# Convolution taps loaded by tap rows, and three small matmul steps each placed one convolution input later, in a two-layer AdaLN/FFN kernel

## What is computed

```python
# layer 0: x -> grouped convolution over positions -> + context -> 1024x1024 FFN with adapters
out = lax.conv_general_dilated(x, weight, (1,), [(4, 4)],
        dimension_numbers=('NCH', 'OIH', 'NCH'), feature_group_count=4)    # 64 -> 64 channels, 9 taps
out = out + (c @ c_weight.T)[:, :, None] + bias[None, :, None]             # context, from cond_128
x = x + (out @ W.T + b + lora(out))
# layer 1: x -> gated mixing of channels -> 64 experts of rank 16, top 16
h = gelu(cond @ W0 + b0); h = gelu(h @ W1 + b1)                            # two gate layers
att = softmax(h @ W2 + b2)                                                 # weights of 8 mixing matrices
y = (sum_k att_k weight_k) @ x + att @ bias_k
x = x + experts(y)
```

## Time and profile before

| | |
|---|---|
| runs before | 649.55, 650.55, 651.34 us |
| profiled execution | 649.2 us, of which the span is 647.4 us (first to last instruction) |
| PE matmuls | 641.3 us busy, 99% of the span |
| PE weight loads | 533.5 us, 82% |
| DVE | 449.0 us, 69% |
| ACT | 214.4 us, 33% |
| POOL | 113.3 us, 18% |
| granted TensorE clock | 0.999 over the span |

### The profile page before, as it was taken

How to read it: one execution, slowest core, us unless ns; L and a number is a source line. 1 busy time by engine, 2 the same in 40 slices (tenths; PEclk the granted TensorE clock), 3 DMA queues, 4 the chain that set the end, 5 groups by cost and what they waited for, 6 DMA issues and landing times.

```text
span 647.4 us, 8392 instructions
## 1 busy us (share of the span) xinstructions
PE 641.3 (99%) x3176; PEld 533.5 (82%) x3176; DVE 449.0 (69%) x695; ACT 214.4 (33%) x278; POOL 113.3 (18%) x143
## 2 busy tenths in 40 slices
PE   8999999999999999999999999999999999999997
PEld 7878888888897888888889788888889888888885
DVE  2758469639378897558769748637967957666685
ACT  2704135324133224335124312324422421334420
POOL 1399760000000220430000121070000020000000
PEclk9999999999999999999999999999999999999999
DMA  8586844985978985776985795377797776047695
GB/s 308 197 310 240 347 127 150 355 268 197 407 252 321 390 327 203 279 227 237 371 309 181 293 374 166 112 222 257 275 330 251 279 260 256 3 131 218 194 347 220
DMA packets 54570, 164.94 MB, mean 255 GB/s; under 512 B 6756, under 2 KB 7652, under 8 KB 54544
## 3 DMA queue, kind: packets, MB, share of 16 engines
q1 hardware_dynamic: 46240, 148.05, 63.5%
q10 hardware_dynamic: 5328, 9.61, 4.7%
q0 software_dynamic: 2976, 6.95, 3.3%
HBM read 138.23 MB, written 26.36 MB: 254 GB/s over the span
## 4 chain that ended last, share of the span: by engine, by line
PE 97%; DMA 1%; DVE 1%; ACT 0%; ACTq 0%; issue 0%; DVEq 0%
PE bank L1519 26%; PE bank L1521 26%; PE bank L1520 26%; PE bank L1533 9%; PE bank L1564 4%; PE bank L1540 2%; PE bank L1570 1%; PE bank L1571 1%; DMA toep<-taps 1%; PE bank L1552 1%; PE bank L1556 0%; PE bank L1558 0%; PE bank L1587 0%; PE bank L1594 0%; DVE work L1067 0%; DVE x L1060 0%
## 5 line engine op out<-in xcount | busy, mean ns | idle before, releaser
L1018 DVE TENSOR_TENSOR piece_lo<-raw,piece_hi 128x1024 fp32r<-128x1024 f32 x60 | 74.5, 1246 | 83.3 <-ACT piece_hi L754 83.3
L1519 PE MATMUL bank<-piece_hi,u_hi 128*128 128x512 f32 x272 | 107.8, 396 | 0.1
L1521 PE MATMUL bank<-piece_hi,u_lo 128*128 128x512 f32 x272 | 107.4, 395 | 0.0
L1520 PE MATMUL bank<-piece_lo,u_hi 128*128 128x512 f32 x272 | 107.3, 394 | 0.0
L754 ACT ACTIVATE piece_hi<-raw 128x1024 fp32r<-128x1024 f32 x60 | 63.3, 1058 | 126.0 <-PE bank L1521 83.9
L1519 PE MATMUL bank<-v_hi,piece_hi 128*128 128x512 f32 x256 | 101.7, 397 | 0.0
L1521 PE MATMUL bank<-v_hi,piece_lo 128*128 128x512 f32 x256 | 101.2, 395 | 0.0
L1520 PE MATMUL bank<-v_lo,piece_hi 128*128 128x512 f32 x256 | 101.0, 395 | 0.0
L1521 PE MATMUL bank<-piece_hi,v_lo 128*128 128x512 f32 x192 | 75.8, 395 | 0.0
L1520 PE MATMUL bank<-piece_lo,v_hi 128*128 128x512 f32 x192 | 75.8, 395 | 0.0
L1519 PE MATMUL bank<-piece_hi,v_hi 128*128 128x512 f32 x192 | 75.8, 395 | 0.0
(11 more groups left out here) (178 smaller groups left out, 822.6 us busy)
## 6 DMA issues: line engine op xcount, KB each, us to landing
raw<-pieces SPq DMA_DIRECT2D x76, 512.0 KB, 5.7
piece_hi<-kept SPq DMA_DIRECT2D x48, 512.0 KB, 5.0
piece_lo<-kept SPq DMA_DIRECT2D x48, 512.0 KB, 6.0
x<-x SPq DMA_DIRECT2D x16, 512.0 KB, 5.6
gate_x<-gates ACTq DMA_DIRECT2D x32, 256.0 KB
out<-x SPq DMA_DIRECT2D x32, 256.0 KB, 4.7
conv_in<-conv_x SPq DMA_DIRECT2D x15, 516.0 KB, 6.9
conv_in<-pieces SPq DMA_DIRECT2D x12, 512.0 KB, 10.1
```

Source lines behind the costliest of these rows:

```text
L1018: dve.tensor_tensor(piece_lo[:, n % SLOTS, :], raw[:, r % RAWS, :], piece_hi[:, n % SLOTS, :].bitcast(F32), ALU.subtract).then_inc(s_piece ...
L1519: pe.matmul(to, left_hi, right_hi, start=first, stop=False)
L1520: pe.matmul(to, left_hi, right_lo, start=False, stop=False)
L1521: return pe.matmul(to, left_lo, right_hi, start=False, stop=last)
```

## The change

`load_taps` takes a tap row in place of a channel group. One call fills 16 partitions, for all four channel groups: its source pattern is 16 channels by 4 groups by 256 numbers, 64 KB. There are eight calls in place of four: ACT's queue issues taps 0 to 3 ahead of the first constants, SP's queue taps 4 to 7 between the conv inputs of entries 0 and 1. One semaphore counts all eight, and PE waits for all of them ahead of entry 0's first convolution. On PE, `context()` and `hidden(0)` stand behind entry 1 in place of entry 0; the spreading of the context and `rest_of_context()` behind entry 2 in place of 1; `hidden(1)` behind entry 3 in place of 2. `logits()` stays behind entry 5. The orders on ACT and DVE stay.

```diff
-        def load_taps(eng, cg):
-            tap, ci = CI, taps.shape[2] * CI
-            windows = bass.AP(taps.tensor, taps.offset + cg * CI * ci, [[tap, PH], [ci, CI], [1, 2 * P]])
-            eng.dma_start(toep[:, cg].rearrange("r h n -> r (h n)"), windows).then_inc(s_taps[cg], 16)
+        def load_taps(eng, tap):
+            ci = taps.shape[2] * CI
+            windows = bass.AP(taps.tensor, taps.offset + tap * CI, [[ci, CI], [CI * ci, CG], [1, 2 * P]])
+            eng.dma_start(toep[tap * CI:(tap + 1) * CI].rearrange("r g h n -> r g (h n)"), windows).then_inc(s_taps, 16)
...
             load_first(0, s_convin[0])
-            load_taps(sp, 1)
-            load_taps(sp, 3)
+            for tap in range(PH // 2, PH):
+                load_taps(sp, tap)
             load_first(1, s_convin_b1)
...
-            load_taps(act, 0)
-            load_taps(act, 2)
+            for tap in range(PH // 2):
+                load_taps(act, tap)
...
+                    if b == 0:
+                        pe.wait_ge(s_taps, 16 * PH)
                     for cg in range(CG):
-                        if b == 0:
-                            pe.wait_ge(s_taps[cg], 16)
                         mm = conv(b, 4 + b % 4, cg)
                     mm.then_inc(s_conv, 1)
-                    if b == 0:
+                    if b == 1:
                         context()
                         hidden(0)
-                    if b == 1:
+                    if b == 2:
                         pe.wait_ge(s_ctx, 2)
...
                         rest_of_context()
-                    if b == 2:
+                    if b == 3:
                         hidden(1)
```

More of the change, by code:

```diff
@@ L160, in adaln_ffn_kernel @@
         s_hidden_w = sem("s_hidden_w")
-        s_taps = [sem(f"s_taps{cg}") for cg in range(CG)]
+        s_taps = sem("s_taps")
         s_later = sem("s_later")
```

## The result

The changed kernel takes 650.92 us (median of 19 runs, 649.78 to 652.91) against 650.03 for the kernel before (19 runs, 648.65 to 651.34). The ratio, which is worked out from all runs and not from the two medians, is 1.0016, with a 95% interval from 1.0009 to 1.0023: slower by 1.0 us, 0.6 to 1.5. This is less than the 0.3% that the prediction called measurable, but no change lies outside the interval. The forecast was 650.5 and no change; the number lies in the range, the sign was not foreseen. That 650.5 came within 0.4 us is in part luck: it was set against the median of three runs, 650.55, and that of nineteen is 650.03.

A forecast was written before the change was run, and what follows sets the result against it. PE, busy 97%, was taken as the bound, with the exponential's chain meeting it before the FFN. PE's 0.95 us gain becomes a wait of about 0.9, net 0.0 on the 650.55 median: 650.5 us, range 649.2 to 652.3.

The forecast's parts named there:

- T: Time at which all taps are loaded, ahead of entry 0's convolution: 5.6 us, bounded by 5.0 and 6.2.
- spread of the context on PE: PE step now behind entries 0, 1, 2: starts at 11.9 us where it was 10.97, 0.9 later.
- DVE's item 0 to item 5: DVE's queue over the convolution items: 7.94 us before, about 7.0 after, item 5 at 20.75 against 20.77.
- first FFN matmul: FFN's start on PE: 24.27 us by the exponential against 24.29 before; 23.3 by PE's chain alone.
- the landing: From the end of the last tap issue to its data: at most 2.3 us, taken from conv input 0.
- the time moves one for one with T: The exponential's chain shifts as T does: net -0.3 to +0.6 us for T between 5.3 and 6.2.
- the slow rival: Tap loads writing 16 partitions are not faster: T 7.4 to 8.6, +1.8 to +3.0 us, 652.3 to 653.5; chance 0.13.
- two chains meet at 24.2 us: Before the FFN, PE's convolutions and ACT's exponential end within 0.1 us, so shortening one alone brings nothing.
- PE's gain would turn into a wait for the exponential: Before the FFN: the 0.95 us PE wins become a wait of about 0.9 us, net 0.0.
- DVE's lost waits: DVE's two stops for PE between items 0 and 5, 0.34 and 0.46 us, both go.
- conv input 1 might come late: Rival: SP's queue reaches this load later and PE stops before entry 1, up to +1.8 us, 652.3; chance 0.07.
- the constants are no cost: Constants land at 9.1 us, `context()` wants them at 9.55 after its move; costed at nothing.

The follow-up runs named there:

- order_only: Kernel before, its taps by channel group, with only the moved steps on PE (context, gate layer one entry later); ratio 1.0014 (1.0006 to 1.0023).
- same_ports: Changed kernel, taps dealt to the queues so that two transfers under way write partitions 32 apart, not 64; 650.77 us, repeated 651.54 us.
- channel_outer: Kernel before and its PE order, partition channel * 8 + tap, so each tap load writes all 128 partitions; ratio 0.9992, both times.
- channel_outer_new: channel_outer with the change's order on PE; ratio to the kernel before 1.0007 (0.9994 to 1.0020).
- rows_only: Changed kernel with PE's old order: new tap loads and one wait for all, no moved steps; ratio 1.0006 (0.9996 to 1.0016).
- rows_only_again: Repetition of rows_only, the changed kernel with PE's old order; ratio 1.0004 (0.9992 to 1.0015).
- channel_outer_late_again: Repetition of channel_outer_late, with the wait for the exponential at the first FFN piece's third row tile; ratio 0.9985 (0.9973 to 0.9997).
- channel_outer_late: channel_outer with PE's wait for the exponential moved to the first FFN piece's third row tile; ratio 1.0000 (0.9985 to 1.0014).
- late_wait: Changed kernel, PE's wait for the exponential moved from before the first FFN piece to its third row tile; ratio 1.0006 (0.9995 to 1.0017).
- changed_again: Changed kernel itself, nothing altered, run once more on the same chip as the second same_ports run; 650.57 us.

## Why the prediction was wrong

Where the numbers stand, step by step:

| step | forecast | measured |
|---|---|---|
| T, all taps there | 5.6 (5.0 to 6.2) | 6.46, 6.34 |
| spread of the context on PE | 11.9 | 12.75 |
| DVE's item 0 to item 5 | 7.0 | 6.89 |
| spread to first FFN matmul | 12.4 | 12.27 |
| first FFN matmul | 24.27 | 25.02 |
| wait in front of it | 0.9 | 0.83 |

**The step that failed is T, and in it the landing.** "I take 5.6, the middle of 5.0 and 6.2": it is 6.46, outside both ends. The other step taken with it, that the time moves one for one with T, then gives 24.27 + 0.86 = 25.13, and 25.02 was measured. Of T's two parts the issue was dearer in my sum than on the chip: the last is over at 3.01, and I had 3.3 to 3.9. The landing was far too cheap: 3.45 us from the end of that issue, where I took at most 2.3. I had the 2.3 from conv input 0, a load of 128 partitions that ran alone.

**What the trace shows in its place** is a line of eight loads and not a last one by itself. By the records of the changed kernel they land one behind another from 4.05 to 6.46, 0.34 us apart, which is some 190 GB/s, while the DMA share is above 1. The last issue ended at 3.01, before the first tap had landed, so what sets T is 512 KB at that rate. The sum had no term for it.

Four forms of the tap loads were run. The rate is that between 4 and 5 us divided by the share there, the packets are the 512 of the taps in each trace's records:

| form | executions | GB/s at a full share | ns for a packet, mean | last tap lands |
|---|---|---|---|---|
| 4 loads, 8 rows outermost, 128 partitions (before, order_only) | 2 | 341, 339 | 51, 56 | 7.42, 7.88 |
| 8 loads of 16 partitions, the change's deal | 5 | 186 to 218 | 69 to 78 | 6.08 to 6.46 |
| 8 loads of 16 partitions, same_ports | 2 | 143, 145 | 88, 93 | 7.12, 7.38 |
| 4 loads, 16 channels outermost, 128 partitions (channel_outer and its variants) | 5 | 201 to 281 | 54 to 68 | 6.20 to 6.88 |

The argument against the slow rival was an error beside it. I wrote that a share of half "is not what a limit at the destination looks like". It isn't, in the old form, where every transfer writes all 128 partitions. It says nothing of a form that writes 16. The rival's numbers (T of 7.4 to 8.6) were too high: T came 0.86 late, about half of the least that it had, 1.8. Its mechanism, narrow transfers at a lower rate, is seen in the packets. That it is what made T late is not shown, since the last form has shorter packets and a last tap no earlier. So the size of the miss is measured and its cause is in part open.

**Right:** that two chains meet at 24.2 us, that PE's gain would turn into a wait for the exponential, its size, and DVE's lost waits. It was off by 0.33 in that the exponential already was the later of the two before. That conv input 1 might come late: it did not in the changed kernel, where entries 0 and 1 run through; it did by 0.43 in channel_outer_new. That the constants are no cost: yes.

**What the change does, in one sum.** Relative to before, the loads alone leave the spread where it was (10.94 in rows_only for 10.97): the stop in the middle has become a later start. The order moves the spread by one entry, +1.8 (12.75 for 10.94), and takes 1.0 out of the way to the exponential (13.3 to 12.3), 0.8 of which are DVE's two waits. Together +0.8, seen as +0.73 in the changed kernel at the FFN's start; the runs say +1.04 with 0.73 inside the interval. All executions with that wait in its old place give the same two distances. From the spread to the first FFN matmul: 13.32, 13.27, 13.27, 13.27, 13.32 in the old order (before, rows_only twice, channel_outer twice) and 12.27, 12.32, 12.31, 12.32, 12.45, 12.24 in the new (the changed kernel twice, order_only, same_ports twice, channel_outer_new).

## What to carry to other kernels

If several chains end at the same place within a few tenths of a us, find the step from which the latest one starts and look where the change puts that step; here it was a matmul of 1 us that three queues hung on, and moving it behind one more piece of work cost more than the removal of a stop of 1 us gave. A burst of loads is costed by the bytes ahead of the last landing and a rate from a row of the same form, not by the landing of one load that ran alone: engines can be fully busy and move less. And where one wait guards a buffer that is only written later, put it there first: it took away a wait of 0.8 us here, and no other took its place.

## What was not expected

- The warm-up of 24 records took 4.32 to 5.49 us over the executions, with the granted clock at 1.00 (the 2.4 GHz level) in every row. In two executions with 5.49 the first convolution, right behind it, was slow at first as well (2.38 and 2.34 us for 16 records, in rows_only_again and channel_outer_late_again, against 1.95); behind a warm-up of 5.35 it was not (1.95 in channel_outer_late). It sets the earliest start of entry 0 anywhere between 5.2 and 6.3 us, which bounds what early taps can give. Its cause is not in the rows.
- The spread of the runs comes partly from one place. Between the first FFN matmul and group 2's convolution lie, by the chain's starts, 309.8 to 310.0 us in ten executions (before, the changed kernel, order_only, late_wait, rows_only_again, both of same_ports and of channel_outer, channel_outer_late), but 310.4 in changed_again, 311.2 in rows_only, 311.1 in channel_outer_new and 310.8 in channel_outer_late_again, with and without each part of the change. In rows_only PE waited for DVE, which waited for ACT, which waited for a weight piece. What makes that piece late stays open. It is as large as the effect under study, so times of a few runs could not have told these kernels apart; the start of the FFN in the trace could.
- The first issue of 1.22 us before has no like after: 0.41 to 0.45 for each of the eight. With 16 channels outermost and 128 partitions (channel_outer) ACT's first took 0.67 and its second 0.62. So being first costs this much only in the form with 8 rows outermost.
